# Attention stage of a fused transformer kernel: 16 reciprocals per token instead of 512, written out on the GpSimd engine, and a new order of the stage's steps

## The reference

```python
# block 1: masked cross attention, 16 heads of 32 channels
x_ = rmsnorm(layernorm(x), norm_w)
q, k, v = (x_ @ wq.T), (ctx @ wk.T), (ctx @ wv.T)          # split into 16 heads
attn = softmax(where(mask, q k^T * 32 ** -0.5, -inf))       # nan -> 0
x = x + tanh(g_xattn[0]) * sigmoid(x_ @ wg.T) * ((attn v) @ wo.T)
# block 2: a layer with ternary weights and 8-bit rounded activations
x = x + tanh(g_ffn[0]) * (round(xn / x_scale) @ w_ternary.T * gamma * x_scale + bias)
# block 3: attention without softmax
x = x + tanh(g_xattn[1]) * (V sigmoid(Q^T K / sqrt(128)))
# block 4: 16 experts, 4 of them for each token, and a shared expert
x = x + tanh(g_ffn[1]) * (experts(x) + shared(x))
```

## Time and profile before

| | us |
|---|---|
| median of three runs | 1333.44 (1332.04 to 1334.49) |
| the profiled execution's own time | 1332.84 |
| its span | 1331.1 |
| PE busy | 1182.3 (89%) |
| DVE busy | 732.8 (55%) |
| ACT busy | 578.8 (43%) |
| POOL busy | 425.0 (32%) |

### The profile page before, as it was taken

One profiled execution on the slowest core, in us unless ns is written; L12 is line 12 of the kernel. 1 busy time (PEld: TensorE's weight loads), 2 busy tenths in 40 slices (PEclk: granted clock), 3 DMA queues, 4 the chain that ended last, 5 costly groups with the idle time before them and its releaser, 6 DMA issues. The chain is left out here.

```text
span 1331.1 us, 24804 instructions
## 1 busy us (share of the span) xinstructions
PE 1182.3 (89%) x7375; PEld 1007.1 (76%) x7388; DVE 732.8 (55%) x1411; ACT 578.8 (43%) x1387; POOL 425.0 (32%) x514
## 2 busy tenths in 40 slices
PE   7697978878877688988999999899999999999995
PEld 6675767767766566766777777789999888999995
DVE  6576665756665698984565664643224543424241
ACT  5453544445445476885211112443334553434342
POOL 1101220210212275630002664244443434443433
PEclk9898989999989898999999999999999999999998
DMA  9000000000010002113000131566446566555454
GB/s 331 28 17 19 3 15 19 1 16 19 1 33 1 8 25 97 33 49 120 33 0 1 66 129 40 176 164 144 78 79 139 149 171 157 134 92 132 84 138 71
DMA packets 54332, 100.31 MB, mean 75 GB/s; under 512 B 5094, under 2 KB 21990, under 8 KB 54262
## 3 DMA queue, kind: packets, MB, share of 16 engines
q0 software_dynamic: 15824, 37.76, 14.7%
q1 hardware_dynamic: 38438, 61.65, 14.1%
HBM read 72.91 MB, written 26.48 MB: 75 GB/s over the span
## 5 line engine op out<-in xcount | busy, mean ns | idle before, releaser
L1896 PE MATMUL t_H<-m_W,t_xT 128*128 128x352 f32 x1632 | 280.3, 327 | 7.2 <-DVE m_W L1974 5.5
L1896 PEld LDWEIGHTS t_H<-m_W,t_xT 128*128 128x128 f32 x1632 | 261.6, 188 | 10.5 <-DVE m_W L1974 7.9
L1864 POOL DMA_INDIRECT out_dram<-t_ys,t_sid x68 | 110.1, 1619 | 221.2 <-ACT t_ys L1925 111.1
L733 ACT ACTIVATE pr<-SC,neg 128x128 f32<-128x128 f32 x256 | 90.9, 373 | 110.4 <-DVE neg L943 110.4
L1941 ACT ACTIVATE t_sl<-t_H 128x352 f32<-128x352 f32 x68 | 31.6, 465 | 173.9 <-PE t_H L1896 173.9
L2019 DVE TENSOR_TENSOR t_hT<-t_TH,t_hT 128x384 fp32r<-128x384 f32 x68 | 37.8, 556 | 101.9 <-ACT t_hT L1962 100.8
L1995 DVE TENSOR_TENSOR t_h<-t_H,t_sl 128x352 f32<-128x352 f32 x68 | 35.6, 524 | 103.5 <-ACT t_sl L1941 103.5
L47 PE MATMUL t_Y<-m_W,t_hT 128*128 128x512 f32 (+1 forms) x207 | 87.7, 423 | 4.9 <-issue 3.0
L1925 ACT ACTIVATE t_ys<-t_Y,t_wcol 128x512 f32<-128x512 f32 x69 | 47.4, 687 | 94.0 <-PE t_Y L49 94.0
L460 POOL TENSOR_TENSOR X<-X,upd 128x512 f32<-128x512 f32 x16 | 20.9, 1308 | 210.1 <-DVE upd L924 210.1
L49 PE MATMUL t_Y<-m_W,t_hT 128*128 128x512 f32 (+1 forms) x207 | 82.1, 397 | 0.0
(11 more groups left out here) (452 smaller groups left out, 3225.6 us busy)
## 6 DMA issues: line engine op xcount, KB each, us to landing
m_raw<-in_L_ffn_w_dram SPq DMA_DIRECT2D x28, 704.0 KB, 5.2
m_raw<-in_L_ffn_w_dram SPq DMA_DIRECT2D x14, 512.0 KB, 4.0
CT<-in_ctx_dram SPq DMA_DIRECT2D x8, 512.0 KB, 3.7
X<-in_x_dram SPq DMA_DIRECT2D x4, 1024.0 KB, 12.9
rows_d<-rows_first SPq DMA_DIRECT2D x16, 256.0 KB, 2.0
out_dram<-X SPq DMA_DIRECT2D x3, 1024.0 KB, 4.3
m_raw<-in_L_ffn_w_dram SPq DMA_DIRECT2D x14, 192.0 KB, 4.1
CT<-in_ctx_dram SPq DMA_DIRECT2D x8, 256.0 KB, 2.7
```

What stands on the lines that cost most here:

```text
L733: i = act.activation(pr[:, t % 2, slot, :], SC[t % HQ][:, slot * S:(slot + 1) * S], ACT.Exp, scale=SCALE0, bias=neg[:, t % 2, slot:slot + ...
L1864: pool.indirect_dma_start(out=m["out_rows"][:, :], out_offset=bass.IndirectOffsetOnAxis(ap=sid[:, b:b + 1], axis=0), in_=ys[:, b, :], in_o ...
L1896: x_ = pe.matmul(bk[b % 2][:, 0:I], xT[:, b % 2, jx, k, :], W13[:, jw, k, j, :], start=k == 0 and jx == jw, stop=k == KC - 1 and jx == 1)
```

## The change

Two things change.

`rc` is done by two engines. VectorE makes 16 reciprocals per token into a new buffer `rec`; POOL then waits for them and writes each one 32 times into `o`; TensorE's `bc` waits for POOL. The buffer `o` may be written again after `oT` of the tile before, a wait that POOL now has; VectorE has instead a wait for POOL's copy of the tile before the last one, since `rec` has two buffers.

All steps of the stage, from the first `S` on, stand in a new order. There are three texts: for group 0 (`first_group`), for groups 1 and 2 (`group`), and for group 3 (`last_group`). What each step does, apart from `rc`, is the same. The list ahead of it (`start`) and behind it (`between`, block 3) is not touched, but three steps of block 3 (`aS.0.0`, with its sigmoid `ag.0.0`, and `qh.1`) stand elsewhere among the steps of the last tiles.

```diff
-        sums, some = sb("sums", [P, 2, NH]), sb("some", [P, 2, NH])
+        sums, some, rec = sb("sums", [P, 2, NH]), sb("some", [P, 2, NH]), sb("rec", [P, 2, NH])
...
-                f"S.1 pv.0 sm.4 v.1 oT.0 uT.-1 {d[3]} sm.5 oP.0 pT.4 mk.2 {d[4]} g.1 pT.5 sm.6 fm.-1 k.1.0 sm.7 k.1.1 nm.4 nm.5 pT.6 sf.-2 {d[5]} k.1.2 "
...
+            "mk.2 cT.3 rc.0 rd.-1 q.1.1 pT.2 u.-2 q.1.2 bc.0 pT.3 q.1.3 sm.4 uT.-2 u.-1 S.1 pv.0 v.1 oT.0 pT.4 k.1.0 sm.5 sm.6 nm.4 "
...
-        plan = steps(start, 0)
-        for g in range(NG):
+        plan = steps(start, 0) + steps(first_group, 0)
+        for g in range(1, NG - 1):
+            plan += steps(group, g)
+        plan += steps(last_group, NG - 1)
...
+                    elif kind == "rc":
+                        pool.wait_ge(o_norm, t + 1)
+                        wait(pool, o_lo, t)
+                        pool.tensor_copy(o[:, :].rearrange("p (h d) -> p h d", h=NH),
+                                         rec[:, t % 2, :].unsqueeze(2).to_broadcast([P, NH, HD])).then_inc(o_wide, 1)
...
-                            pe.wait_ge(o_norm, t + 1)
+                            pe.wait_ge(o_wide, t + 1)
...
-                        wait(dve, o_lo, t)
+                        wait(dve, o_wide, t - 1)
...
-                        dve.reciprocal(o[:, :].rearrange("p (h d) -> p h d", h=NH), some[:, t % 2, :].unsqueeze(2).to_broadcast([P, NH, HD])).then_inc(o_norm, 1)
+                        dve.reciprocal(rec[:, t % 2, :], some[:, t % 2, :]).then_inc(o_norm, 1)
```

More of the change, by code:

```diff
@@ L232, in attention_and_ternary @@
                  "W.o Wh.o Wl.o q.0.2 q.0.3 ")
-        during = {0: ("sx.4 sx.5 sx.6 sx.7", "xa.1", "fq.0 xb.1", "xd.1", "ft.0 fq.1 fg.0", "ft.1 fq.2 fg.1",
-                      "sx.8 sx.9 ft.2 sx.10 sx.11 fg.2", "fq.3 sx.12 sx.13 sx.14 sx.15 xa.2", "ft.3 xb.2 fg.3", "xd.2")}
-        plan = steps(start, 0)
-        for g in range(NG):
[L237 to L242, removed]
-                f"S.1 pv.0 sm.4 v.1 oT.0 uT.-1 {d[3]} sm.5 oP.0 pT.4 mk.2 {d[4]} g.1 pT.5 sm.6 fm.-1 k.1.0 sm.7 k.1.1 nm.4 nm.5 pT.6 sf.-2 {d[5]} k.1.2 "
[L244 to L249, removed]
[8 rows of a table removed]
-            "oP.3 uT.0 u.1 fm.0 ", NG - 1)
+        first_group = (
[7 rows of a table added]
+        group = (
[6 rows of a table added]
+        last_group = (
[6 rows of a table added]
+        plan = steps(start, 0) + steps(first_group, 0)
+        for g in range(1, NG - 1):
+            plan += steps(group, g)
+        plan += steps(last_group, NG - 1)
         between = {2: "uT.-3", 3: "sf.-4", 4: "fm.-3 st.-2", 6: "st.-1", 8: "ra.-1 sf.-3", 10: "rb.-1", 12: "rd.-1 u.-2", 17: "uT.-2",
@@ L317, in attention_and_ternary @@
         s_fill, s_out, p_exp = (sem(n) for n in ("s_fill", "s_out", "p_exp"))
-        o_norm, o_hi, o_lo = (sem(n) for n in ("o_norm", "o_hi", "o_lo"))
+        o_norm, o_wide, o_hi, o_lo = (sem(n) for n in ("o_norm", "o_wide", "o_hi", "o_lo"))
         added, biased, q_step, f_step, some_ok = (sem(n) for n in ("added", "biased", "q_step", "f_step", "some_ok"))
```

## The result

The kernel after takes 1236.8 us (median of 4 runs, 1235.11 to 1236.93) where the kernel before takes 1333.0: a ratio of 0.9274 with a 95% interval of 0.9258 to 0.9291, 7.3% faster. The forecast was 1256 and its range 1240 to 1292. The direction was right, and so were the old waits that go; the gain is 96 us where 77 were forecast, and the time is 3 us under the range's lower end.

The account below looks back on a forecast made before the run. TensorE was taken to bound the stage: 329 us of work at full clock, 24 idle and 3 of slow clock make 356 instead of 433.4. Thus 1332.84 - 77 = 1256 us, range 1240 to 1292 for 8 in 10.

Parts of the forecast that it names:

- What bounds the stage: Whole changed stage: TensorE, 346.7 of 433.4 us busy, is limited by 86.7 us idle and 18 of slow clock, floor 329.
- The reciprocals: In `rc`: 16 reciprocals take 0.26 us instead of 3.35, POOL's copy 0.8; VectorE is freed of 50 us.
- The chain's leeway: Behind `rc`, on the way to `bc`: about 1.4 us a tile of delay can be absorbed.
- Each old wait: TensorE's waits for reciprocals, `fu`, `oT`: 1 us left at tile 0, 2 of 16.6 for `fu`, 2 of 15.9 for `oT`.
- What is late next: Walk through the new lists, tiles 4 to 7: 2 us late a group; with allowances 5, 4, 4, 11 idle, 24 in all.
- The clock: TensorE's granted clock in the stage: idle pieces of about 1 us make slow clock cost 3 us instead of 18.
- Elsewhere: Outside the stage: block 3 and the experts' stage keep their lists and times.
- its lower end: Lower end of the main case, 1243 us: a stage with 11 us idle instead of 24.
- Table loads: ScalarE in the tail: two more table loads, 2.6 us, from sigmoids between exponentials, counted within the last group's 11 us idle.
- The port: Rival: POOL's 16 copies and VectorE hold each other up, 16 x 1.0 = 16 us, giving 1272; chance 0.13.
- Half the order: Rival: new waits in unfollowed chains leave 56 us idle, slow clock costs 8, giving 1293; chance 0.14.
- The dear copy: Rival: POOL's repeated read is slow; at 6.2 us a copy the gain is gone, at 8 us 1362; chance 0.05.

Follow-up runs that it names:

- e6: The kernel after with POOL's copy made 4 times per tile, each waiting for the one before: 1256.29 us, ratio 0.9439 to the kernel before.
- e9: The kernel after with POOL's copy made 8 times per tile, each waiting for the one before: 1315.52 us, ratio 0.9864 to the kernel before.
- e3 to e5: Three runs of the kernel after with the old order except in group 0 (1280.85 us), groups 1 and 2 (1278.48 us), or group 3 (1283.82 us).
- e14: The kernel after with the gate projections of tiles 12 and 13 ahead of the next tile's scores, not behind them: 1237.31 us, ratio 0.9279.
- e13: The kernel after with the scores of tiles 13 and 14 right ahead of the previous tile's pv, as before the change: 1236.28 us, ratio 0.9278.
- e8: The kernel after with block 3's first sigmoids (`ag.0.0`) moved behind the last exponentials and last gate: 1233.33 us, ratio 0.9253.
- e7: The kernel after with VectorE instead of POOL writing the 16 reciprocals out to 512 columns: 1239.60 us, ratio 0.9294.

## Why the prediction was right or wrong

**What bounds the stage: right.** TensorE's idle time and its slow clock were named as the 104 us above a floor of 329. Busy time fell to 326.4 at clock 1.00, and 92.8 of the 433.4 us went.

**The reciprocals: right.** 0.26 us for 16 of them, measured 0.253. The copy at 0.8 us, taken near POOL's cast of 0.61, is 0.611: it should have been taken at the cast itself. VectorE's 50 us less are 47. The chain's leeway of 1.4 us is 1.3 by e6's idle time and 1.7 by e9's.

**Each old wait: right in place, near in size.** Left for the wait at tile 0: 1, measured none. For `oT`: 2, measured 1.7. For `fu`: 2, measured 1.3. Group starts 87 us apart: 83.6, 87.0 and 87.6. e3 to e5 confirm, to some 4 us in 66, that groups can be reckoned one by one.

**What is late next: the step that failed, in size.** The prediction left 24 us idle, 5 + 4 + 4 + 11; measured are 3.3, 2.7, 2.7 and 5.6, 14.2 in all. For groups 1 and 2, the 2 us that came from following the steps, with 2 more for what had not been seen, were too much by 1.3 us each. And the 2 us are near the 2.7 by luck: of the three kinds that the walk named, group 1 has waits of 0.4 (exponentials), 0.2 (`fu`) and none (`oP`). In their place are 1.2 us at the key quarter behind the ternary product (see the profile after), which the walk had not found, 0.4 for POOL's copy at the group's first tile and 0.3 for a gate. The 11 us of the last group were not followed step by step but judged from the missing projections. It was measured at 5.6. The new order keeps gates back behind the next tile's scores (e14) and issues scores early (e13), which fills 3.2 of the 5.4 us between them, and both could be read in the lists beforehand; what fills the rest stays open.

**The clock: undersized.** Idle pieces of about 1 us were said to cost 3 us still; they cost nothing, PEclk is 1.00 in all four groups. And what it had cost before was 346.7 - 326.4 = 20 us, not 18. Together 5 to 6 us.

**Elsewhere: no change was forecast, and 3 us are there.** The first scores are at 35.11 instead of 35.85, and the stretch behind the stage is 859.5 us instead of 861.9. As that stretch wanders over more than 6 us with next to nothing changed in it, the difference can't be put to the change.

So of the 19 us missed, 10 are the idle time, 6 the floor and the clock, 3 the rest. The range failed for the same reason: its lower end varied one term, the idle time, and kept the others at their middle. With 11 us idle it gave 1243; with the 14.2 measured and the floor and the clock as measured the stage alone gives 1240, the very end of the range. The 3 us that put the time below it come from outside the stage and can't be credited to anything.

**Table loads: right.** Two more, in the tail; with the sigmoid that brings them they cost 2.0 us by e8.

**The rivals.** The port: its mechanism is there; the copies' price of up to 16 us is not (e7). Half the order: no. The dear copy: its point of decision was put at 6.2 us and lies near 6.3 by the line through e6 and e9, though by two errors that cancel: the gain to be eaten was larger (96 us, not 77), and the rival had no term for the slow clock that comes with long waits, 29 us of the 79 in e9. Its leeway was about right.

## What to carry to other kernels

Price an order by two things: the busy time of the engine with most work at its full clock, and a walk through the new lists that asks at each hand-over what stands between. Do the walk for the odd group as well as for the regular one, since an allowance in its place was the largest error here; and check that the walk's places, not only its sum, are the ones that wait. And when several terms are uncertain in the same direction (idle time, clock, floor), the end of a range needs all of them at their end, as a shorter wait brings a faster clock with it.

## What the runs showed of the hardware

- TensorE's clock made two halves of a change worth more together than apart: 26.4 and 49.7 us of stage alone, 92.8 together, and 12.2 of the 16.7 us beyond the sum are busy time. With waits of at most 1.2 us the granted clock stayed at 1.00 for 340 us; behind one of 1.85 us (e14) it was 0.72 for 6 us; with 54 us of waits in 16 pieces (e9) it was 0.91, and the same work took 29 us more.
- POOL reads 16 numbers 32 times each and writes 512 columns in 0.61 us, as fast as its plain cast of 512; VectorE does it in 0.43 (e7), as fast as its rounding of 512 plain columns (`fu<-fu`, 0.43 in the same run). So the repeated read costs neither anything that shows.
- A normalised tile `xn` took VectorE 1.59 us beside POOL's sum of two 128x512 operands (1.29 us) and 0.45 to 0.55 elsewhere. Beside POOL's copy (0.61 us) `fu` took 0.89 to 0.96 us, and 0.54 to 0.55 without it (e7).
- The stretch behind the stage, the same code in all kernels but for a transpose, lasted between 855.3 and 861.9 us in the profiled runs. An edit worth 2 us in its own stretch (e8) can't be seen in the whole time against that; it has to be read in its stretch.
